# Attention's middle turns written out, and TensorE's side work dealt out one piece a step

## The reference, cut to what matters

```python
h = _L0_tok_ref(x, L0_tok_W, L0_tok_b)               # patches @ W + b, 64 x 196 tokens of 192
h = h + _L0_attn_ref(_layernorm(h), Wq, Wk, Wv, Wproj)
h = h + _L0_ffn_ref(_layernorm(h), ...)
# attention: 12 heads of 16
q, k = apply_rope(q, cos, sin), apply_rope(k, cos, sin)
scores = jnp.einsum('bhsd,bhtd->bhst', q, k) / math.sqrt(hd)
weights = jnp.where(mask, jax.lax.erf(scores) + 1.0, 0.0)
denom = jnp.maximum(weights.sum(axis=-1, keepdims=True), EPS)
y = jnp.einsum('bhst,bhtd->bhsd', weights, v) / denom
return y.transpose(0, 2, 1, 3).reshape(B, S, D) @ Wproj.T
```

## Time and profile before

| | |
|---|---|
| time, median of 3 runs | 3662.2 us (3652.69 to 3668.25) |
| the profiled execution's own time | 3660.63 us |
| its span, first to last instruction | 3658.8 us |
| turns 1 to 28 (the loop), 119.03 to 1587.35 us | 1468.32 us, 52.44 us a turn |
| turn 29, 1587.35 to 1640.71 us | 53.36 us |
| mean granted TensorE clock over the span | 0.871 |

### The profile page before, as it was taken

The page is one execution under the profiler, slowest core; times in us unless marked ns, Lnnn a source line. Parts: engine busy times, 40 slices in busy tenths (PEclk is TensorE's granted clock), DMA queues, the critical chain, the costliest instruction groups (busy, mean ns, idle before and its releaser), DMA issues. The chain is left out here.

```text
span 3658.8 us, 76656 instructions
## 1 busy us (share of the span) xinstructions
PE 3342.6 (91%) x26932; PEld 2322.6 (63%) x26932; DVE 2467.0 (67%) x4826; ACT 1601.6 (44%) x3287; POOL 1385.5 (38%) x1170
## 2 busy tenths in 40 slices
PE   5999999999999999998239999899999999999997
PEld 4777777767777777776125555556666565665665
DVE  5988888889889988888655555454544445454443
ACT  2444444434444444443004444444544445454443
POOL 0222222222222222222205554135555555555554
PEclk8887788778777887785559999999999999999999
DMA  3332233233323332321111222213323232332222
GB/s 96 72 70 70 68 83 69 60 77 82 68 60 80 83 69 58 80 56 40 52 51 58 72 72 72 83 34 64 59 43 63 39 63 39 64 62 42 39 40 31
DMA packets 330574, 227.45 MB, mean 62 GB/s; under 512 B 209103, under 2 KB 309551, under 8 KB 326159
## 3 DMA queue, kind: packets, MB, share of 16 engines
q1 hardware_dynamic: 259536, 163.94, 17.6%
q0 software_dynamic: 57472, 48.46, 8.9%
q10 hardware_dynamic: 13262, 10.65, 0.8%
HBM read 107.75 MB, written 67.85 MB: 48 GB/s over the span
## 5 line engine op out<-in xcount | busy, mean ns | idle before, releaser
L1279 DVE SCALAR_TENSOR_TENSOR ffn_hidden<-ffn_up,ffn_silu 128x490 f32<-128x490 f32 (+2 forms) x534 | 350.5, 670 | 775.1 <-ACT ffn_silu L1260 730.9
L699 POOL TENSOR_TENSOR weights<-weights,x_pair 128x400 f32<-128x400 f32 x384 | 396.0, 1031 | 915.2 <-DVE weights L563 754.8
L1260 ACT ACTIVATE ffn_silu<-ffn_gate 128x490 f32<-128x490 f32 (+2 forms) x534 | 301.7, 583 | 795.1 <-PE ffn_up L1223 776.0
L1431 POOL DMA_INDIRECT out_rows<-done,ids x256 | 417.2, 1630 | 507.5 <-ACT done L1535 408.3
L1244 PE MATMUL ffn_out<-ffn_w_hi,ffn_hidden_hi 128*126 128x192 f16 (+2 forms) x2124 | 530.3, 250 | 4.9 <-ACT done L1535 3.1
L615 DVE RECIPROCAL recip<-x_product 128x200 f32<-128x200 f32 x384 | 534.4, 1392 | 0.0
L1245 PE MATMUL ffn_out<-ffn_w_lo,ffn_hidden_hi 128*126 128x192 f16 (+2 forms) x2124 | 522.6, 246 | 0.0
L1246 PE MATMUL ffn_out<-ffn_w_hi,ffn_hidden_lo 128*126 128x192 f16 (+2 forms) x2124 | 522.6, 246 | 0.0
L750 PE MATMUL bank<-w_qkv,normed_t 96*128 96x192 f32 (+1 forms) x1024 | 395.5, 550 | 19.1 <-ACT normed_t L413 19.1
L1272 DVE TENSOR_TENSOR ffn_hidden_lo<-ffn_hidden,ffn_hidden_hi 128x490 f16<-128x490 f32 (+2 forms) x534 | 356.4, 668 | 16.3
L1254 ACT CAST ffn_hidden_hi<-ffn_hidden 128x490 f16<-128x490 f32 (+2 forms) x534 | 320.9, 601 | 105.7 <-DVE ffn_hidden L1279 103.7
(11 more groups left out here) (180 smaller groups left out, 7301.2 us busy)
## 6 DMA issues: line engine op xcount, KB each, us to landing
patches<-in_patches SPq DMA_DIRECT2D x32, 1176.0 KB, 5.2
ffn_raw<-in_w SPq DMA_DIRECT2D x18, 768.0 KB
dram_x_t<-x_t SPq DMA_DIRECT2D x32, 392.0 KB, 3.0
x_t<-dram_x_t SPq DMA_DIRECT2D x24, 512.0 KB
base<-dram_h SPq DMA_DIRECT2D x24, 384.0 KB, 4.1
out_rows<-sums ACTq DMA_DIRECT2D x24, 384.0 KB, 4.4
v_held<-v SPq DMA_DIRECT2D x64, 102.0 KB, 2.3
dram_h<-h SPq DMA_DIRECT2D x32, 192.0 KB
```

The costliest lines, as they stand in the source:

```text
L699: nc.gpsimd.tensor_tensor(weights[:, n % 4], weights[:, n % 4], x_pair[:, n % 4, ::-1], ALU.mult)\
L1260: nc.scalar.activation(T.silu[:, m % 2, 0:n], T.gate[m % 2][:, 0:n], ACT.Silu, scale=1.0 / (TOKEN_SCALE * WEIGHT_SCALE)).then_inc(T.silued, 1)
L1279: nc.vector.scalar_tensor_tensor(T.hidden[:, m % 2, 0:n], T.up[m % 2][:, 0:n], HIDDEN_SCALE / (TOKEN_SCALE * WEIGHT_SCALE), T.silu[:, m % ...
L1431: nc.gpsimd.indirect_dma_start(out=dram["out"][:, :], out_offset=bass.IndirectOffsetOnAxis(ap=ids[i][0:height, t, 0:1], axis=0), in_=done[ ...
```

## The change

Two things are done at once.

1. The hardware loop goes. All 29 mid turns are written out, on all five engines, so u is a number everywhere and no register holds a semaphore's count.
2. PE's side work is dealt out anew, and the order of the bank queue with it: tokens at steps 1, 2, 9 and 10; LN1T and QK tile 0 at 3; QK tile 1 and YT at 4; PROJ at 5; QK tiles 2 and 3 at 6 and 7; all values at 8; X2T at 9; ROUTE at 11. ACT's copies follow; its casts move from steps 6 and 7 to 7 and 10. DVE rotates in steps 4 and 7, and does the subtraction (L652) in steps 7 and 10. SP's queue is put in the order in which these things now come ready: the stores of `h2` and `x2`, the transposes of image 0, `v_held`, `x2_t`, the transposes of image 1, the logits.

No instruction of computing is added or removed.

```diff
-LN1T, QK, VV, YT, PROJ, X2T, ROUTE, TOK = (
-    (0, 1), (2, 3, 4, 5), (6, 9), (7, 8), (10, 11), (13, 14), (16,), (12, 15))
+    (1, 2), (3, 4, 9, 10), (11, 12), (5, 6), (7, 8), (13, 14), (16,), (0, 15))
+QK_STEPS = (3, 4, 6, 7)
...
-    with eng.Fori(0, (MIDS - 1) // 2) as j:
-        turn("mid", 2 * j + 1, j, 1)
-        turn("mid", 2 * j + 2, j, 0)
+    for u in range(1, MIDS):
+        turn("mid", u, (u - 1) // 2, u % 2)
...
 # TensorE
-                    if n in (3, 4) and has_next:
-                        for t in range(2 * n - 6, 2 * n - 4):
-                            out = room(QK[t])
-                            product(out[:, 0:2 * D], normed_t, t, qkv_w, 2 * D).then_inc(full[QK[t] % NB], 1)
-                    if n in (4, 5) and has_next:
-                        pos = VV[n - 4]
+                    if n in QK_STEPS and has_next:
+                        t = QK_STEPS.index(n)
+                        out = room(QK[t])
+                        product(out[:, 0:2 * D], normed_t, t, qkv_w, 2 * D).then_inc(full[QK[t] % NB], 1)
+                    if n == 8 and has_next:
+                        for k, pos in enumerate(VV):
...
-                    if n in (7, 8) and has_tokens:
-                        tokens(n - 7)
-                    if n == 11 and has_tokens:
-                        tokens(2)
-                        tokens(3)
+                    if n in (1, 2, 9, 10) and has_tokens:
+                        tokens(n - 1 if n < 3 else n - 7)
...
 # ScalarE: casts of the rotated queries and keys
-                    if n in (6, 7) and has_next:
-                            act.wait_ge(qk_turned[n - 6][slot], ...)
+                    if n in (7, 10) and has_next:
+                            act.wait_ge(qk_turned[n // 10][slot], ...)
...
 # VectorE: subtraction, then rotation
+                    if n in (7, 10) and has_next:
+                        for t in range(n // 10 * 2, n // 10 * 2 + 2):
+                            dve.wait_ge(qk_hi, 8 * u + 8 + 2 * t + 2)
-                    if n in (3, 4) and has_next:
+                    if n in (4, 7) and has_next:
```

More of the change, by code:

```diff
@@ L69 @@
 QKU = 2 * QKS
-VECTOR_STEPS = 74
 class Tally:
@@ L158, in parts_of, with turns @@
             kind in ("mid", "late", "last", "end"), kind in ("pre", "pro", "first", "mid"))
-def turns(eng, turn):
+def turns(turn):
     turn("pre", -2, 0, 0)
@@ L340, in turn, with turn_rotated @@
                       .then_inc(patches_in[prev], 16)
+                def turn_rotated(image):
+                    sp.wait_ge(roped, 4 * u + 6 + 2 * image)
+                    sp.sem_inc(x2t_spacer, 1)
+                    for b in range(2):
+                        rows = (NEAR, FAR16)[b]
+                        sp.dma_start_transpose(turned_columns(qk_t[prev], image * QKS + b * NEAR, rows),
+                                               rotated_rows(qk, 2 * image + b, rows)).then_inc(qk_turned[image][prev], 16)
+                if has_prev:
+                    sp.wait_ge(x2_ready, 4 * u)
+                    sp.sem_inc(x2t_spacer, 1)
+                    for b in range(2):
+                        sp.dma_start(image_rows(dram["h2"], u - 1, b), tile_rows(h2[prev], b)).then_inc(rows_out[prev], 16)
+                        sp.dma_start(image_rows(dram["x2"], u - 1, b), tile_rows(x2[prev], b)).then_inc(rows_out[prev], 16)
+                if has_next:
+                    if has_prev:
+                        sp.wait_ge(scored, PAIRS * u)
+                        sp.sem_inc(x2t_spacer, 1)
+                    turn_rotated(0)
                 if has_next:
@@ L353, in turn @@
                         sp.dma_start(held, part).then_inc(held_in[prev], 16)
[L354 to L377, removed]
                 if has_prev:
@@ L388, in turn @@
                     sp.dma_start(dram["logits"][:, bass.ds((u - 1) * UT, UT)], logits[prev][:]).then_inc(logits_out[prev], 16)
-            turns(sp, turn)
+            turns(turn)
             for s in range(2):
@@ L490, in turn @@
                         copy_out(ROUTE[0], logits[prev][:], E)
-            turns(act, turn)
+            turns(turn)
             act.wait_ge(zeroed, 48)
@@ L669, in turn @@
                     multiply_x(u + 1, 0)
-            turn("pre", -2, 0, 0)
-            turn("pro", -1, 0, 1)
-            turn("first", 0, 0, 0)
-            with dve.Fori(0, (MIDS - 1) // 2) as j:
-                chain.enter(j, VECTOR_STEPS)
-                turn("mid", 2 * j + 1, j, 1)
-                turn("mid", 2 * j + 2, j, 0)
-            chain.leave((MIDS - 1) // 2)
-            closing_turns(turn)
+            turns(turn)
         @block.gpsimd
@@ L710, in turn @@
                         root(1, last_root(kind, u))
-            turns(pool, turn)
+            turns(turn)
         @block.tensor
@@ L873, in attend @@
                 last.then_inc(attended, 1)
-            turns(pe, turn)
+            turns(turn)
 def routing(nc, dram, slot_of, entry, T):
```

70 lines of the change are left out of this document (35 added, 35 removed).

## The result

The changed kernel took 3719.63 us in the median of 5 runs (3697.51 to 3786.45), the kernel before, measured beside it, 3663.32 us (5 runs, 3652.69 to 3679.97). The ratio, which leaves out the slow execution of 3786.45 us, is 1.0139, with a 95% interval of 1.0113 to 1.0165: it is 1.4% slower, where 3.4% faster was forecast. Its executions lie further apart than those of the kernel before, and the profiled one is the longest of them, 125.8 us over the profiled one of before. A second profile of the same kernel comes with the last experiments; it has the same kinds of turn in another mixture.

What follows compares the result with a forecast made beforehand. Attention had PE and DVE near their limits. Turns falling from 52.44 to 48.2 us gain 118.7, turn 29 5.2, sum 123.9 off 3660.6: 3536.7, or 3538 for the median; main range 3516 to 3564, with the late-PE rival to 3600.

Steps and rivals of the forecast that it cites:

- PE fits in: Attention's middle turns: PE's 40.0 us of work at clock 0.86 takes 46.5 us, within the forecast turn of 48.2.
- get dense products ahead of QK: Steps 1 and 2, bare and in the low stretch before, get token products that help bring the clock back; no separate size.
- The reading of the turns before: Turns 1 to 29: thirteen behind a branch average 55.8 us at 0.74 to 0.77, the others 49.5 at 0.85 or 0.86.
- the clock stays low: Rival, chance 0.06: spread work leaves PE short gaps and no long run; clock 0.72, 57.1 us a turn, 3796 us.
- the code doesn't stream: Rival, chance 0.04: written-out code pauses PE once a turn, all turns 54.5 us, 3720 us in all.
- The loop's pauses: Thirteen branches go, with 28.2 us of PE standing still and the low clock behind them; at most 82 us gained.
- The dealing-out: PE's side work spread over the steps, so DVE waits less for PE; some 42 us of the gain.
- DVE's floor of 47.8 us, 48.2 with waits: Each turn: DVE busy 46.63 us plus 1.20 of small waits and settles, plus 0.4 of waits for PE.
- The casts of step 7: DVE's subtraction waits for ACT's casts behind QK tile 3: 1.3 us a turn, nothing if PE has its lead.
- SP's queue: Image 0's transposes start behind step 7's subtraction and take 7.0 us, hidden within 12.4 with 5 us over.
- First and last turns, 0 give or take 5: Time of the first and last turns, outside turns 1 to 29: no change, give or take 5 us.
- PE's work as "40.0 us at the full clock": PE's work per turn: 50.06 us busy at mean clock 0.80 is 40.0 us at the full clock, used as a price.

Runs made afterwards that it cites:

- first kernel: Against the kernel before the change: the loop written out, the side work left at its old steps; 3623.64 us, ratio 0.9894.
- fifth kernel: Against the changed kernel: token tiles 0 and 1 both in step 2, right ahead of the queries, 2 and 3 still at 9 and 10; 3524.79 us, 0.9629.
- tenth kernel: Token tiles 0 and 1 both in step 2, changed by moving DVE's division of image 1's last sums from step 1 to 2; 3556.59 us, no ratio.
- fourth kernel: Against the changed kernel: token tile 0 in step 1 and tile 2 in step 9 each computed twice; 3548.76 us, 0.9709.
- the two last: Pair in step 2, sums divided in step 2; then either queries' tiles 0 and 1 both in step 3, or tile 0 twice there; 3519.73 and 3520.27 us.
- the thirteenth: Against the kernel with the pair and the sums' division in step 2: queries' and keys' tiles at steps 3, 3, 6, 7; 3519.73 us, 0.9599.
- the fourteenth: Against the kernel with the pair and the sums' division in step 2: queries' tile 0 computed twice in step 3; 3520.27 us, 0.9605.

## Why the prediction was wrong

**The step that failed** is "PE fits in: 40.0 us of work, at the 0.86 of the better turns, is 46.5 us". It took the clock as a property that the better turns lend to all. Measured in the profiled execution is a clock of 0.71, and PE busy for 56.4 us a turn (1579.33 / 28). The clock follows from where the pieces stand, and the change moved just these. The ground given, that steps 1 and 2 "get dense products ahead of QK", did not carry: with one tile a step and the backbone between, the clock comes up at the start of the turn and holds in some turns (17), and falls again in others (11) at PE's first tile of queries. With the tiles doubled in steps 1 and 9 (0.97), or the pair in step 2 (0.93), it stays up through PE's heavy steps in nearly all turns. The reading of the turns before was too neat as well: turns 14 and 20, with no branch ahead of them, took 52.1 us at 0.79 and not the 0.85 or 0.86 that the prediction gives for all such turns, so the low clock was not the branch's alone.

The rival "the clock stays low" had the mechanism, at a chance of 0.06. It gave 0.72 and 57.1 us a turn; measured are 0.71 and 57.3 in the profiled execution, though 3719.63 us for its 3796 in the median, since executions hold different shares of long turns (the second profile of the changed kernel: 53.8 a turn). That it hits the profiled execution so well is in part luck, as is the other rival's 3720 us ("the code doesn't stream"): the pauses which that one needs are not in the trace. The Trainium skill's advice (TensorE: Matmul & The Clock Gate, Why this matters for your kernels) against gaps was cited there; gaps are not what these traces show, since PE is busy in all of the 40.96 us at 1.2 GHz.

**Point by point.**

- *The loop's pauses.* Right: none of PE's waits of that kind is left in the turns. "Up to 82" for it measured 38 us (first kernel, against 3661.88), 36 and 46 (with the new places). The rest was lost because turns without a branch still alternate 49.0 and 53.4 us with the clock; the prediction had seen such a turn in turn 29.
- *The dealing-out, "some 42" of gain.* Measured: 96 us of loss. Of its parts the tokens' move was right in sign (71), the spread of queries, keys and values wrong (138 lost), but worth 70 once the pair stands in step 2.
- *DVE's floor of 47.8 us, 48.2 with waits.* Near: 48.83 in turn 17, and 47.77 a turn in the fifth kernel. But the floor is lower, as the tenth kernel's 46.94 shows (DVE is busy 45.97 us a turn in the fifth kernel, 0.66 less than before the change, which the prediction held fixed), and the fifth kernel's turns settle at 47.78 for another reason (see the last section). That 47.8 agrees with it is luck.
- *The casts of step 7.* Forecast at nothing with PE's lead, 1.3 us without: 1.83 us in turn 11, 43.9 over 28 turns, and 0.0 where the clock was up (the fourth kernel). Here too the lead was the assumption.
- *SP's queue.* Right: PE waited 0.6 us in all for the transposed queries and keys.
- *First and last turns, 0 give or take 5.* 8.7 us less ahead of turn 1, a small miss.
- *PE's work as "40.0 us at the full clock".* Busy time times clock is no constant: for the same instructions it is 60.75 x 0.64 = 38.9 us in turn 11 and 47.95 x 0.95 = 45.6 in turn 17. One reason is that the side work nearly doubles at 1.2 GHz while the backbone grows by 1.39 (2.07 for 1.49). So even with the clock given, 40.0 / clock was no safe price.

**Shown and not shown.** Shown: that the clock, by the pieces' places, makes the difference (with work only added, the fourth kernel is 171 us faster, and the waits go with the low clock); and which half of the change does harm. Not shown: what the clock answers to in step 3. Windows of the changed kernel: the low stretch at the start of turn 11, and the one at 2.4 GHz behind it; the same two of turn 16; the low stretch at the start of turn 17:

```profile
686.57:688.67 2.10, 2.10 (x13) 1.41 (x14) 2.10 (x5) 0.00 (x0) 1.45 (x2) 0.50 0.00 0
688.67:695.49 6.82, 6.16 (x68) 5.13 (x69) 5.18 (x13) 3.29 (x7) 1.17 (x2) 1.00 0.48 177
980.57:982.21 1.64, 1.64 (x6) 1.25 (x4) 1.64 (x3) 0.00 (x0) 1.46 (x2) 0.50 0.00 0
982.21:989.04 6.83, 6.17 (x74) 5.13 (x74) 5.11 (x14) 3.29 (x7) 1.03 (x1) 1.00 0.50 179
1042.07:1043.65 1.58, 1.58 (x7) 1.52 (x5) 1.58 (x3) 0.00 (x0) 1.46 (x2) 0.50 0.00 0
```

In turn 11 the low clock ends 2.10 us behind the turn's start, in turn 16 1.64 us, in turn 17 1.58 us. Turns 11 and 16 lose the clock again and take 61.4 and 61.5 us; turn 17 keeps it for 40.96 us and takes 48.8. The same holds for the others: in both profiles, turns with the rise at 1.46 to 1.58 us keep the clock, and those with it at 1.62 to 2.17 lose it (so do the two of the first profile with it at 0.70, 9 and 19). So 0.06 us in where the rise falls goes with 12.7 us of turn. A gap of PE's doesn't tell them apart: ahead of the first tile of queries PE stands still 0.66 us for `normed_t` in turn 11 and in turn 17 alike:

```profile
694.85 2.27 PE L742 MATMUL bank<-w_qkv,normed_t 96*128 96x384 f32 x4 [0.66 <-ACT normed_t L413]
...
1050.56 1.53 PE L742 MATMUL bank<-w_qkv,normed_t 96*128 96x384 f32 x4 [0.66 <-ACT normed_t L413]
```

That the place of the rise decides is read from many turns of one code, and was not set by an experiment.

## What to carry to other kernels

Where TensorE's clock varies within a turn, a piece of work has no fixed price: before pieces are dealt out evenly, look in which steps the clock is up and what stands ahead of them, and try the densest piece right ahead of the heavy steps; here that place was worth 195 us against the same pieces one step apart. A cheap test is to compute dense pieces twice: if the kernel gets faster, placement is worth more than work. One piece may not be enough to show it (40 us with one tile, 171 with two). And compare turn by turn, not in the mean: turns of several lengths from one code are the sign, and so are executions that lie far apart.

## What was not expected of the hardware

- Adding 24 products a turn to the changed kernel saved 171 us, 4.6%.
- Clock levels hold on: 40.96 us at 1.2 GHz with PE busy all the time, on the same instructions that run at 2.4 GHz for 40.96 us in another turn. The Trainium skill (TensorE: Matmul & The Clock Gate, Part 1: The HAM clock gate) says that the point of rising varies from run to run with the monitor's phase; the traces agree: turn 1 of the changed kernel took 57.36 us at a clock of 0.66 in one profiled execution and 46.95 at 1.00 in the other.
- Three different kernels (the fifth and the two last) settle at the same 47.78 us a turn, though DVE waits mainly for `y_sum` in the fifth and for `x_pair` in the thirteenth. It is no engine's limit, since the tenth kernel has turns of 46.94. In each of the three the clock's rise comes at one place of most turns: 2.67 us behind its start in the fifth (580.27 to 582.94 us above), 3.2 us in the other two. In the fourteenth one sees them settle: its turns 1 to 4 take 46.94, 47.27, 47.52 and 47.65 us while the rise comes 1.35, 2.20, 2.71 and 2.98 us behind their starts, and at 3.24 us the turn takes 47.78 and the rise stays there. A later rise leaves PE more work at 1.2 GHz and lengthens the turn, until turn and clock repeat together; that this is the reason is an inference from these rows.
